# A graph network kernel on one core: gathers straight from the packed edges, and another order of the work ahead of the matrix build

## The reference

```python
h = maximum(layernorm(x), 0)
x = x + two_layers(h)      # per layer: sum of l2norm(h)[src] over each dst (plus itself),
                           # l2norm, times norm(h), @ Wl + bl, plus h @ Wr, l2norm
h = maximum(layernorm(x), 0)
x = x + unet(h)            # gcn_conv in; 3 x (gcn_conv, batch norm, relu, keep the top half of the
                           # nodes by a score); bottom conv; 3 x (unpool, join, gcn_conv, norm, relu); out
```

## Time and profile before

| what | value |
|---|---|
| three runs | 1072.91, 1073.50, 1074.96 us; median 1073.5 |
| the profiled execution | 1074.95 us; its span, first to last instruction: 1073.2 us |
| TensorE busy | 919.2 us, 86% of the span |
| VectorE busy | 609.1 us, 57% |
| ScalarE busy | 404.7 us, 38% |
| GpSimd busy | 69.5 us, 6% |
| mean granted TensorE clock | 0.938 of full speed |
| `edge_table<-edges`, one of its two copies | 4656 KB |

### The profile page before, as it was taken

One profiled execution on the slowest core, in us unless ns is written; L12 is line 12 of the kernel. 1 busy time (PEld: TensorE's weight loads), 2 busy tenths in 40 slices (PEclk: granted clock), 3 DMA queues, 4 the chain that ended last, 5 costly groups with the idle time before them and its releaser, 6 DMA issues.

```text
span 1073.2 us, 17179 instructions
## 1 busy us (share of the span) xinstructions
PE 919.2 (86%) x6997; PEld 594.6 (55%) x6997; DVE 609.1 (57%) x1603; ACT 404.7 (38%) x897; POOL 69.5 (6%) x91
## 2 busy tenths in 40 slices
PE   0548999999999999999999988988876767777997
PEld 0436666866855558665555554664435434444654
DVE  4699999996929933653121383834533644525321
ACT  1868999982660011651020220942105311221200
POOL 2100000000000000000000002240024100020000
PEclk9779999999899999999999988998997896889999
DMA  6500000008910020020000006952114100141002
GB/s 182 161 28 2 2 1 2 2 2 311 404 52 1 1 60 2 2 83 39 1 2 1 1 1 141 320 140 104 34 52 109 47 1 1 31 184 64 2 1 61
DMA packets 42592, 70.59 MB, mean 66 GB/s; under 512 B 3630, under 2 KB 30529, under 8 KB 41992
## 3 DMA queue, kind: packets, MB, share of 16 engines
q1 hardware_dynamic: 34418, 48.41, 13.6%
q0 software_dynamic: 4176, 17.86, 5.3%
q10 hardware_dynamic: 3910, 3.12, 1.1%
HBM read 33.08 MB, written 41.09 MB: 69 GB/s over the span
## 4 chain that ended last, share of the span: by engine, by line
PE 59%; DVE 28%; DMA 5%; ACT 3%; issue 3%; POOL 1%; DVEq 0%; SPq 0%; ACTq 0%; POOLq 0%
PE psum L3001 25%; DVE region L1041 7%; DVE region L1034 7%; PE psum L2526 6%; PE psum L2414 6%; PE psum L2755 3%; PE psum L2491 2%; PE psum L2319 2%; DVE region L1626 2%; PE psum L2952 2%; DMA edge_table<-edges 2%; PE psum L2344 1%; PE psum L2823 1%; DMA region<-in_src 1%; PE psum L2983 1%
## 5 line engine op out<-in xcount | busy, mean ns | idle before, releaser
L3001 PE MATMUL psum<-adj,region 128*128 128x448 fp8e4 x1050 | 202.6, 353 | 0.1
L3001 PEld LDWEIGHTS psum<-adj,region 128*128 128x128 f16 x1050 | 102.7, 98 | 93.1 <-DVE region L1819 0.5
L2344 PE MATMUL psum<-region 128*128 128x200 bf16 (+2 forms) x1176 | 110.1, 228 | 25.7 <-DVE region L1041 25.6
L2344 PEld LDWEIGHTS psum<-region 128*128 128x128 bf16 x1176 | 92.6, 99 | 60.0 <-DVE region L1041 31.2
L1984 ACT ACTIVATE adj<-psum 128x400 fp8e4<-128x400 f32 x196 | 86.6, 518 | 21.3 <-PE psum L2348 20.7
L3001 PE MATMUL psum<-region 128*128 128x448 fp8e4 (+2 forms) x426 | 84.3, 360 | 11.9 <-DVE region L1819 11.9
L2319 PE MATMUL psum<-adj,region 128*128 128x448 fp8e4 x350 | 92.1, 356 | 0.0
L1041 DVE TENSOR_TENSOR region<-iota_key,region 128x1200 bf16<-128x1200 bf16 x147 | 91.1, 670 | 0.0
L2142 ACT ACTIVATE region<-psum 128x512 fp8e4<-128x512 f32 (+6 forms) x111 | 62.0, 598 | 71.6 <-PE psum L2983 25.8
L1034 DVE TENSOR_TENSOR region<-iota_lo,region 128x3072 bf16<-128x3072 bf16 x49 | 85.4, 1744 | 0.4 <-PE psum L2348 0.2
L1845 DVE SCALAR_TENSOR_TENSOR region<-psum,unfit,region 128x448 f32<-128x448 f32 (+2 forms) x31 | 19.4, 661 | 113.5 <-PE psum L3001 96.9
(11 more groups left out here) (375 smaller groups left out, 1280.7 us busy)
## 6 DMA issues: line engine op xcount, KB each, us to landing
both_table<-adj SPq DMA_DIRECT2D x1, 10000.0 KB, 28.8
adj_table<-adj SPq DMA_DIRECT2D x1, 10000.0 KB, 54.8
edge_table<-edges SPq DMA_DIRECT2D x1, 4656.0 KB
region<-dk_dram SPq DMA_DIRECT2D x2, 1568.0 KB, 8.1
adj_table<-region SPq DMA_DIRECT2D x1, 2704.0 KB, 9.0
half_table<-region SPq DMA_DIRECT2D x2, 832.0 KB, 5.4
both_table<-region SPq DMA_DIRECT2D x1, 1650.0 KB, 10.7
xs_dram<-nodebuf SPq DMA_DIRECT2D x1, 1600.0 KB, 5.2
```

The source lines that it names most:

```text
L2344: pe.matmul(psum[:, q % BUILD_BANKS, i * KEYS + k0:i * KEYS + k1], hot_lo[:, r, c, j, :, i], hot_key[:, r, c, j, k0:k1, i], start=(n == 0) ...
L3001: last = pe.matmul(psum[:, b, 0:width], here[:, t, k, :], rows, start=(t == 0 and k == 0), stop=(t == n_src - 1 and k == 1))
```

## The change

- `edge_table` and its copies go. The gathers index `edges` itself, seen as rows of 32 words (`edge_windows`), and wait only for the write of the packed words. Each fetches 384 words from its start.
- ScalarE's queue waits for both edge loads before it loads x.
- On VectorE the 25 comparisons and `row_i` come before the statistics of x, and the edge keys before the norms. The low part's subtraction moves from ahead of batch 0 into the loop, ahead of batch 3 (SPLIT_BATCH).
- On ScalarE `keep_edges` for all groups comes right behind the square, then the evictions of the transposed h0, the scaling of all 25 tiles, the high part, and then the release of the six build banks. The first count waits for the low part.
- On TensorE the key transposes come before those of h0.
- Thirteen loads of weights move from ScalarE's queue to SyncE's.
- The keys need no spare buffer: `dest` is written over the gathered words.
- In the poolings TensorE waits at each of the first ScalarE units for its own bank only, and a copy of the staged skip sums (`skip_total`) moves behind the first half of the turns.

```diff
@@ -197,7 +198,7 @@
-        edge_table = dram("edge_table", (ROWS, SLOTS), I32)
+        edge_windows = edges.rearrange("(n o) -> n o", o=GRAIN)
@@ -665,11 +665,21 @@
             sp.wait_ge(table_in, DMA)
-            for r0, r1 in ((0, ROWS // 16 * 16), (ROWS // 16 * 16, ROWS)):
-                rows = bass.AP(edges.tensor, r0 * GRAIN, [[GRAIN, r1 - r0], [1, SLOTS]])
-                sp.dma_start(edge_table[r0:r1, :], rows).then_inc(table_in, DMA)
+            sp.dma_start(weights[:, 0, :], a["L1_gnn_in_W"]).then_inc(weights_in, DMA)
...
             sp.wait_ge(parts0_ready, 1)
+            sp.dma_start(wl0[:], a["L0_gnn_Wl0"]).then_inc(w2_ready, DMA)
...
@@ -797,9 +807,9 @@
             pool.wait_ge(rows_known, 1)
-            pool.wait_ge(table_in, 3 * DMA)
+            pool.wait_ge(table_in, DMA)
             for g in range(GROUPS):
-                pool.indirect_dma_start(out=edge_rows[:, g, :], out_offset=None, in_=edge_table,
+                pool.indirect_dma_start(out=edge_rows[:, g, :], out_offset=None, in_=edge_windows,
@@ -975,6 +985,11 @@
+            dve.wait_ge(more_consts, 2)
+            for c in range(LASTS):
+                nc.vector.tensor_scalar(later[:, c, :], iota_window[0:EP, :], last_f[:, c:c + 1], None, ALU.is_gt).then_inc(windows_compared, 1)
+            dve.wait_ge(windows_counted, 1)
+            nc.vector.tensor_scalar(row_i[:].rearrange("p (g o) -> p g o", o=1), psum[:, 4:4 + GROUPS, 32:33], float(ROWS - 1), None, ALU.min).then_inc(rows_known, 1)
             dve.wait_ge(x_in, 2 * DMA)
...
@@ -1016,12 +1021,14 @@
             for g in range(GROUPS):
                 edge_keys(g)
+            dve.wait_ge(h0_squared, 1)
+            step(nc.vector.tensor_reduce(ss, tiles(region3[:, 0:PAD]), AX.X, ALU.add))
+            inverse_norms(unit, norm0, ss)
+            nc.vector.tensor_scalar(unit, unit, UNIT_SCALE, None, ALU.mult).then_inc(scaled0, 1)
...
-            dve.wait_ge(hi0_ready, 1)
-            nc.vector.tensor_tensor(parts0[:, :, 1, :], tiles(region3[:, PAD:2 * PAD]), parts0[:, :, 0, :], ALU.subtract).then_inc(parts0_ready, 1)
@@ -1030,6 +1037,9 @@
                 if b >= 2:
                     dve.wait_ge(pair_done, (b - 1) * BATCH_PAIRS)
+                if b == SPLIT_BATCH:
+                    dve.wait_ge(hi0_ready, 1)
+                    nc.vector.tensor_tensor(parts0[:, :, 1, :], tiles(region3[:, PAD:2 * PAD]), parts0[:, :, 0, :], ALU.subtract).then_inc(parts0_ready, 1)
@@ -1898,6 +1908,7 @@
             act.wait_ge(pads_zeroed, 1)
+            act.wait_ge(edges_in, 2 * DMA)
             load_x(act, x_in)
@@ -1936,33 +1939,25 @@
+            for g in range(GROUPS):
+                keep_edges(g)
+            for g, (t0, n) in enumerate(GROUPS4):
+                act.wait_ge(h0_turned, g + 1)
+                nc.scalar.activation(h0t[:, t0 * P:(t0 + n) * P], psum[:, 4 + g % 3, 0:n * P], ACT.Copy).then_inc(h0t_ready, 1)
             act.wait_ge(scaled0, 1)
-            scale_nodes(0, 12)
-            keep_edges(0)
-            scale_nodes(12, TILES)
-            keep_edges(1)
-            act.wait_ge(scaled0, 3)
+            scale_nodes(0, TILES)
+            act.wait_ge(scaled0, 2)
             nc.scalar.activation(parts0[:, :, 0, :], tiles(region3[:, PAD:2 * PAD]), ACT.Copy).then_inc(hi0_ready, 1)
-            for g in range(2, GROUPS):
-                keep_edges(g)
             act.sem_inc(bank_free, BUILD_BANKS)
-            act.wait_ge(parts0_ready, 1)
...
-                if n > 0:
+                if n == 0:
+                    act.wait_ge(parts0_ready, 1)
+                else:
                     act.wait_ge(excess_ready, n)
@@ -2163,9 +2158,6 @@
-                    if p == 2:
-                        copy(skip_total[0][:, 0:4 * BLOCK], skip_stage).then_inc(skip_out, 1)
@@ -2189,6 +2181,7 @@
                                 else:
+                                    copy(skip_total[0][:, 0:4 * BLOCK], skip_stage).then_inc(skip_out, 1)
                                     keep_skip()
@@ -2784,8 +2776,6 @@
-                pe.wait_ge(skip_out, SKIP_OUT[0 if below == 0 else 2])
@@ -2813,6 +2803,8 @@
+                    if e == 0 and u // 2 < TURN_BANKS:
+                        pe.wait_ge(skip_out, (0 if below == 0 else SKIP_OUT[1]) + bank + 1)
```

More of the change, by code:

```diff
@@ L60 @@
 BATCH_PAIRS = BATCH // 2
+SPLIT_BATCH = 3
 HOT_STEPS = 1 + CHUNKS
@@ L667, in _ @@
             sp.wait_ge(table_in, DMA)
-            for r0, r1 in ((0, ROWS // 16 * 16), (ROWS // 16 * 16, ROWS)):
-                rows = bass.AP(edges.tensor, r0 * GRAIN, [[GRAIN, r1 - r0], [1, SLOTS]])
-                sp.dma_start(edge_table[r0:r1, :], rows).then_inc(table_in, DMA)
-            sp.wait_ge(parts0_ready, 1)
+            sp.dma_start(weights[:, 0, :], a["L1_gnn_in_W"]).then_inc(weights_in, DMA)
+            sp.dma_start(weights[:, 1:4, :], a["L1_gnn_dn_W"].rearrange("s k f -> k s f")).then_inc(weights_in, DMA)
+            sp.dma_start(weights[:, 4, :], a["L1_gnn_bot_W"]).then_inc(weights_in, DMA)
+            sp.dma_start(weights[:, 5:11, :], a["L1_gnn_up_W"].rearrange("s (h k) f -> k (s h) f", h=2)).then_inc(weights_in, DMA)
+            sp.dma_start(weights[:, 11, :], a["L1_gnn_out_W"]).then_inc(weights_in, DMA)
+            sp.wait_ge(parts0_ready, 1)
+            sp.dma_start(wl0[:], a["L0_gnn_Wl0"]).then_inc(w2_ready, DMA)
+            sp.dma_start(wr0[:], a["L0_gnn_Wr0"]).then_inc(w2_ready, DMA)
+            sp.dma_start(wl1[:], a["L0_gnn_Wl1"].rearrange("(m k) f -> k m f", m=2)).then_inc(w2_ready, DMA)
+            sp.dma_start(wr1[:], a["L0_gnn_Wr1"].rearrange("(m k) f -> k m f", m=2)).then_inc(w2_ready, DMA)
+            sp.dma_start(bias0[:], row_of(a["L0_gnn_bl0"]).broadcast_to((P, 256))).then_inc(w2_ready, DMA)
+            sp.dma_start(bias1[:], row_of(a["L0_gnn_bl1"]).broadcast_to((P, P))).then_inc(w2_ready, DMA)
+            sp.dma_start(scales[:, 0:1], row_of(a["L0_gnn_scale0"]).broadcast_to((P, 1))).then_inc(w2_ready, DMA)
+            sp.dma_start(scales[:, 1:2], row_of(a["L0_gnn_scale1"]).broadcast_to((P, 1))).then_inc(w2_ready, DMA)
             sp.wait_ge(h0t_ready, len(GROUPS4))
@@ L991, in _ @@
             nc.vector.scalar_tensor_tensor(shift, shift, -0.5, inv, ALU.mult, ALU.mult).then_inc(centered, 1)
[L993 to L1002, removed]
             def edge_keys(g):
                 dve.wait_ge(gathered[g], DMA)
-                low, high, dest = (work[3 * (g % 2) + k].bitcast(I32) if 3 * (g % 2) + k < 5 else spare_work.bitcast(I32) for k in range(3))
+                low, high, dest = work[2 * (g % 2)].bitcast(I32), work[2 * (g % 2) + 1].bitcast(I32), edge_rows[:, g, :]
                 loc = key_rows[:, g, :]
@@ L1907, in _ @@
             act.dma_start(vec_rows[V_OUT_B:V_OUT_B + 1, :], row_of(a["L1_gnn_out_b"])).then_inc(weights_in, DMA)
[L1908 to L1912, removed]
             act.wait_ge(centered, 1)
@@ L1920, in _ @@
             nc.scalar.activation(region3[:, 0:PAD], nodebuf[:], ACT.Square).then_inc(h0_squared, 1)
-            for g, (t0, n) in enumerate(GROUPS4):
-                act.wait_ge(h0_turned, g + 1)
-                nc.scalar.activation(h0t[:, t0 * P:(t0 + n) * P], psum[:, 4 + g % 3, 0:n * P], ACT.Copy).then_inc(h0t_ready, 1)
             def scale_nodes(t0, t1):
@@ L1937, in keep_edges @@
                                          ACT.Copy).then_inc(by_edge_ready, 1)
-            act.wait_ge(scaled0, 1)
-            scale_nodes(0, 12)
-            keep_edges(0)
-            scale_nodes(12, TILES)
-            keep_edges(1)
-            act.wait_ge(scaled0, 3)
+            for g in range(GROUPS):
[3 more added lines that the diff above has]
+                nc.scalar.activation(h0t[:, t0 * P:(t0 + n) * P], psum[:, 4 + g % 3, 0:n * P], ACT.Copy).then_inc(h0t_ready, 1)
+            act.wait_ge(scaled0, 1)
+            scale_nodes(0, TILES)
+            act.wait_ge(scaled0, 2)
             nc.scalar.activation(parts0[:, :, 0, :], tiles(region3[:, PAD:2 * PAD]), ACT.Copy).then_inc(hi0_ready, 1)
-            for g in range(2, GROUPS):
-                keep_edges(g)
             act.sem_inc(bank_free, BUILD_BANKS)
-            act.wait_ge(parts0_ready, 1)
[L1950 to L1954, removed]
-            act.dma_start(bias1[:], row_of(a["L0_gnn_bl1"]).broadcast_to((P, P))).then_inc(w2_ready, DMA)
-            act.dma_start(scales[:, 0:1], row_of(a["L0_gnn_scale0"]).broadcast_to((P, 1))).then_inc(w2_ready, DMA)
-            act.dma_start(scales[:, 1:2], row_of(a["L0_gnn_scale1"]).broadcast_to((P, 1))).then_inc(w2_ready, DMA)
             adj_dests = adj[:, :].rearrange("p (t n) -> p t n", t=TILES)
@@ L2287, in _ @@
             pe.wait_ge(rows_known, 1)
-            pe.wait_ge(h0_ready, 1)
-            for g, (t0, n) in enumerate(GROUPS4):
-                if g >= 3:
-                    pe.wait_ge(h0t_ready, g - 2)
-                for t in range(t0, t0 + n):
```

(11 more changed lines are left out.)

2 lines of the change are left out of this document (removed).

## The result

| | median (lowest to highest) | runs |
|---|---|---|
| before | 1074.64 us (1072.91 to 1074.96) | 5 |
| after | 1068.00 us (1066.75 to 1069.76) | 5 |

The ratio is 0.9948, with a 95% interval of 0.9929 to 0.9968: the change saves about 5.6 us (3.4 to 7.6; the two medians differ by 6.6). I forecast 1075.0 and a range of 1070 to 1079: the time lies outside it. The profiled execution took 1066.75 us (span 1064.9, mean granted clock 0.950), against 1074.95 (1073.2, 0.938).

The account below looks back on a forecast made before the run. TensorE leads the chain over the whole span, but VectorE bounds the build, whose start a row of transfers sets. Start +4.4 and poolings -2.9 gave +1.5 us on the median 1073.5: forecast 1075.0, range 1070.0 to 1079.0.

Parts of the forecast that it names:

- banks free at 64.3: Ahead of the build: ScalarE releases the six build banks at 64.3 us, and TensorE waits for them before its first pair.
- Edges first, x behind them: Loads at the start: edges in at 9.9 us rather than 13.6; x, held up by the packed-edge write, at 22.8.
- the rival (in by 19): Load of x: not held up, in at 18.2 to 19 us; net -2.6 us, 1070.9; chance 25%.
- the slower one (x later than 23.4): Load of x: small loads and weights on the same engines delay it to 25.3 us; net +4.0, 1077.5; chance 15%.
- Comparisons ahead of the statistics: VectorE before the build: comparisons and row_i done at 18.3 us while x is awaited, costing nothing; x centered at 30.8.
- No table: Before the edge keys: two transfers go (17.5 us in the chain); gathers in by about 27 us, 4 us to spare.
- ScalarE's line: ScalarE from x centered to the release of the six build banks, all in one line: sum 34.0 us, taken as 33.5.
- the rival of gathers in pieces: Edge gathers: each row of 384 fetched in 12 pieces, 38 us per gather, 21 us late, 1096; chance 5%.
- the rival that it runs ahead: Bank release: doesn't wait for the high-part copy's end, TensorE starts up to 2.8 us earlier; net -1.3, 1072.2; chance 15%.
- Low part at batch 3, queues: Build: subtraction (3.5 us) not hidden, batch 3 ends at 77.9, start loses 4.4 us; moving DMAs between queues gains nothing.
- the mark: In the build: end of VectorE's batch 3, the start of batch 4; 73.48 us before, forecast 77.9.
- Poolings: Both poolings: first turns start 1.1 and 2.1 us earlier through fewer bank waits; gain 2.9 us, bounds 0 and 5.0.

Follow-up runs that it names:

- x at once: The changed kernel with the load of x no longer waiting for the edge loads; ratio 0.9986 (0.9977 to 0.9996) to the kernel before, in set 2.

## Why the prediction was wrong

It was wrong in sign and by some 7 us in size: -5.6 measured, +1.5 forecast. The step that failed is "banks free at 64.3": TensorE had them by 57.55. Its largest parts are a release that does not wait for the copy before it (2.8 us) and a line of work on ScalarE priced 2.8 us too long; x 1.3 us early is the rest. By its own steps:

- *Edges first, x behind them.* Edges at 9.9, measured 9.22; x at 22.8, measured 21.54. 1.3 us too late: 0.7 are the edges, the rest x's own load. That x is held up is right: it took 12.2 us from its issue, where alone it takes 8.2, and the rival (in by 19) fell, as did the slower one (x later than 23.4). That the write does it is shown in part only: with the write on more engines too it still took 10.8 (6.11 to 16.95).
- *Comparisons ahead of the statistics.* Done at 18.3, measured 17.56, with x awaited. Right, and they cost nothing, as said. I did not see that without the wait for the edges the result would be the same.
- *No table.* The gathers had time to spare and ScalarE's line was what came last. Right: the keys start at 29.46 with no wait. That the table's 17.5 us gain nothing by themselves is shown by the run with that edit alone (-0.68). There a gather takes 3.4 us from issue to landing (median of four), 3.1 before, so the rival of gathers in pieces fell.
- *ScalarE's line.* Here the first size failed. "Together 11.0" for keys and h0 was 7.9 (42.21 to 50.10), and most of that is the 25 transposes of h0: 3.65 us, where I had 6.4. Two things were wrong. I divided the 1.54 us of a row of six transposes by six; the row of twelve above took 2.79, so six more cost 1.25, which is 0.21 each, and some 0.28 comes once per row. That makes 5.5 for the 25. The other 1.9 us I put down to the clock: I priced all of them at the low one, and TensorE doubled its rate among them (last section). With scaling at 7.3 instead of 7.5, the line from ReLU to the end of the high part took 30.7. My terms add up to 34.0; that I took 33.5 has no reason in the text, and it brought the number nearer by luck. Against 33.5 the miss is 2.8 us.
- *The release in "banks free at 64.3".* This part failed as a mechanism. I counted the release behind the high-part copy in order, and gave the rival that it runs ahead 15%. It does: 2.8 us, and 2.9 with the wait put in. No row of before showed it either way, and my only argument for order was that the instruction stands there; the 15% was too little for that.
- *Low part at batch 3, queues.* As forecast: from the banks' release to the mark 13.5 us, forecast 13.6. The first count waited 1.0 us for the subtraction, but TensorE, which waited for VectorE's tiles until 71.16, lost nothing by it.
- *Poolings.* First turns 1.1 and 2.1 us earlier: measured 0.75 to 1.05 and 2.06 where no gather came late; with one late (the second profile of the changed kernel) the first turn came 0.9 us later than before. In sum -2.9, measured -3.8 and -3.5, which their intervals don't tell apart.
- *Its signs.* Edges at 9.22, the subtraction between batches 2 and 3, and the first turns came as forecast. The first build matmul (57.55, forecast 63.5 to 65, behind the copy) and batch 4 (71.02, forecast 77 to 79) did not; the statistics missed their 22 to 23.5 by 0.5. Before batch 2 VectorE was idle 4.8 us, not ten. And of the signs of being wrong one came true: in two of three profiles of the changed kernel the first turn of the first pooling waited for a gather.

The mark closes: 77.9 - 1.3 (x) - 2.8 (ScalarE's line) - 2.8 (release) = 71.0, measured 71.02. Only the release was switched by a run of its own; the other two terms are read from rows. With -2.5 there and -3.6 in the poolings the sum is -6.1, within all three intervals of the changed kernel.

The range failed for one reason: the three errors of the start lie one behind the other on one path, and all had the same sign. I priced x and the release as separate rivals, each with everything else at its forecast, and gave ScalarE's line none, so the range never held two at once.

## What to carry to other kernels

Taking a long transfer out of the chain is worth what the next line behind it lets through; look at the order of the instructions behind it first, and change both. A row that shows a long transfer on five of 16 engines is to be followed up before anything is reordered round that transfer: here it was worth 4.4 us, the reordering 2.5. Where several unsure terms lie in series on one path, let the range hold their sum, not the largest of them.

## What the hardware did that I had not expected

- A semaphore increment that stands by itself behind a long ScalarE instruction runs while that instruction is still at work: TensorE went ahead 0.17 us after a 2.87 us copy had started, and so in every profile that has the release there, 0.16 or 0.17 us (57.38 and 57.55; 52.96 and 53.13; 57.26 and 57.42). With a wait for the copy's own increment put before it, it is 3.06. It follows that such an increment says nothing on whether the data are ready: that signal has to hang on the instruction that writes them. A release of a resource that is long free can use it.
- TensorE transposed twice as fast at an unchanged reading of the clock. The changed kernel, windows of 42 to 45 and 47 to 49 us (after the times: PE, PEld, DVE, ACT, POOL busy, granted clock, DMA share, GB/s):

```profile
42.00:45.00 3.00, 2.26 (x11) 2.29 (x12) 2.75 (x1) 2.70 (x8) 0.00 (x0) 1.00 0.00 0
...
47.00:49.00 2.00, 2.00 (x20) 1.81 (x17) 1.76 (x11) 2.00 (x5) 0.00 (x0) 1.00 0.00 0
```

  0.21 us each, then 0.10, both under 1.00. The trace has no clock record before about 47 us, and the view shows 1.00 there. The run "x at once" has records for the same transposes:

```profile
42.00:45.00 3.00, 1.84 (x9) 1.87 (x10) 2.33 (x1) 2.85 (x7) 0.00 (x0) 0.50 0.00 0
...
47.00:49.00 2.00, 2.00 (x19) 1.74 (x17) 1.69 (x11) 2.00 (x5) 0.00 (x0) 1.00 0.00 0
```

  0.20 us each at 0.50, which is 1.2 GHz, and 0.105 at 1.00. So the first reading of 1.00 above is no measurement: TensorE worked there at the lower of its two levels.
- The kernel before took 22 us more in one set of runs than in two others. In the profile of that set which has its poolings, the first 655 us were 1.0 us late, and by 850 us, behind the second pooling's turns, it was 22.4.
